# Two recurrent networks side by side: the first network's state update moved ahead of the second's gate sums on VectorE, and the second bf16 part of the state taken by GpSimd

## The chip, the cores and the metric

The kernel runs on one core of one Trainium2 chip. The metric is the device time of one execution in microseconds (us). A core has five engines that run their own programs and meet through semaphores: TensorE (PE in the rows; PEld is its weight load), VectorE (DVE), ScalarE (ACT), GpSimd (POOL) and SyncE (SP, which starts transfers here).

## The reference, cut to what matters

The whole program is a decoder of four layers, twelve stages. Only the first piece of the first stage is touched: two LSTM networks (one gives queries, one gives keys) that run over the same normalised input, 8 sequences of 112 positions with 256 features, with a state of 256.

```python
def _lstm(x, Wih, Whh, b):
    xW = jnp.einsum('bsd,gd->sbg', x, Wih) + b
    h0 = jnp.zeros((x.shape[0], Whh.shape[1]), x.dtype)
    def step(carry, xt):
        h, c = carry
        gates = xt + h @ Whh.T
        i, f, g, o = jnp.split(gates, 4, axis=-1)
        c = jax.nn.sigmoid(f) * c + jax.nn.sigmoid(i) * jnp.tanh(g)
        h = jax.nn.sigmoid(o) * jnp.tanh(c)
        return ((h, c), h)
    _, hs = jax.lax.scan(step, (h0, h0), xW)
```

Each of the 112 steps needs the state of the step before it, for each network. The two networks (l = 0 and l = 1 in the code) do not depend on each other.

## The kernel before, in words

`Recurrence` holds the stage. The input part `xW` of all gates is computed first (until about 70 us). Then 112 steps t follow, with both networks in each. The state is kept transposed: 128 partitions by 16 (two halves of 256 features, 8 sequences).

The product `h @ Whh.T` needs nearly fp32 accuracy and is made of bf16 matmuls. The state is split into three parts, each the upper 16 bits of an fp32 number: `h[:, 0]` is the state itself, `h[:, 1]` is what its upper half leaves out, and `h[:, 2]` what the upper half of `h[:, 1]` leaves out. `upper` is the bf16 view of the upper halves. The weights are split into three bf16 parts as well. For one network and one step TensorE runs three groups of 16 matmuls (L1323), named `part` 2, 1 and 0: part 2 reads only `h[:, 0]`, part 1 also `h[:, 1]`, part 0 also `h[:, 2]`. So the first group waits for the state (`h_hi`), the second for the middle part (`h_mid`), the third for the last (`h_parts`). TensorE's program is network 0's 48 matmuls, then network 1's 48, then the next step. The sixth gate block of the last group signals `gates_full`, the eighth signals it again.

VectorE sums the four slots of PSUM for the first six gate blocks and then for the last two (`dve_gates`, TENSOR_REDUCE at L1422, 48 and 16 outputs per partition). ScalarE takes tanh of both (L1352, L1355; the sigmoids are made from tanh) and writes the next step's input part to PSUM (L1366). VectorE makes the cell (`dve_cells`, L1428 and L1431), ScalarE its tanh (L1359), and VectorE the new state `h[:, 0]` (`dve_state`, L1440, signals `h_hi`). In the kernel before, VectorE then also makes `h[:, 1]` (`dve_middle`, L1446, signals `h_mid`), and GpSimd makes `h[:, 2]` (L1383, signals `h_parts`) and a halved copy of the state for later stages (L1385, signals `h_kept`, which the same network's next state waits for).

The order of each engine's program is written out by hand and is kept strictly: an instruction that waits holds back everything behind it on its engine. In VectorE's program of one step, network 1's first sum stands between network 0's cell and network 0's state.

Of the kernel before, what the change touches and what calls it, by code (L numbers as in the profile page):

```python
# [313 lines left out]
def norm_half_dve(k, half, src, xn, xT, before):  # L314

    norm_half_rows(k, half, src, xn, before)
    norm_half_turned(k, xT, before)
# [28 lines left out]
def norm_half_pool(k, before):  # L346
    s, G, st = k.s, k.nc.gpsimd, k.stats4
    G.wait_ge(*s.stat_ready(before + 1))
    G.tensor_tensor(st[:, :, 9], st[:, :, 8], k.minus_half[0:S, :].broadcast_to([S, HALF]),
                    ALU.pow).then_inc(*s.rstd_ready.up())  # L350
# [17 lines left out]
class Attention:  # L368
# [433 lines left out]
    def pool(self):  # L802
        k, s, G = self.k, self.s, self.nc.gpsimd
        self.pool_begin()
        norms = 0
        for step, b, i in self.order():
            u = self.bufs[b % 2]
            if step in ("stats", "ln", "stats3"):
                norms += 1
                G.wait_ge(*s.stat_ready(norms))  # L810
                G.tensor_tensor(k.stats[:, 9:10], k.stats[:, 8:9], k.minus_half[0:S, :],  # L811
                                ALU.pow).then_inc(*s.rstd_ready.up())
            elif step == "qm":
                G.wait_ge(*s.q_ready(b + 1))
                tiles, per = self.q.shape[1], self.qm.shape[1]
                for t in range(tiles):
                    ins = G.tensor_tensor(u["qm"][:, t * per:(t + 1) * per, :],
                                          self.q[:, t, :].unsqueeze(1).broadcast_to([P, per, S]),
                                          self.qm.unsqueeze(2).broadcast_to([P, per, S]), ALU.mult)
                ins.then_inc(*s.qm_ready.up())  # L820
            else:
                self.pool_more(step, b, i, u)
# [431 lines left out]
class Recurrence:  # L1254
# [113 lines left out]
    def pool(self):  # L1368
        k, s, G = self.k, self.s, self.nc.gpsimd
        for half in range(2):  # L1370
            norm_half_pool(k, half)
        G.wait_ge(*k.landed["l0a_whh"].now())
        for l in range(2):
            G.wait_ge(*s.whh_a(2 * l + 1))
            G.tensor_tensor(self.raw[:, l], self.raw[:, l], self.whh[:, 0, l], ALU.subtract).then_inc(*s.whh_g.up())
            G.wait_ge(*s.whh_a(2 * l + 2))
            G.wait_ge(*s.whh_g(2 * l + 1))
            G.tensor_tensor(self.whh[:, 2, l], self.raw[:, l], self.whh[:, 1, l], ALU.subtract).then_inc(*s.whh_g.up())
        for t in range(S):
            for l in range(2):  # L1380
                h, upper = self.h[:, l], self.upper[l]
                G.wait_ge(*s.h_mid(2 * t + l + 1))
                G.tensor_tensor(h[:, 2], h[:, 1], upper[:, 1], ALU.subtract).then_inc(*s.h_parts.up())  # L1383
                G.wait_ge(*s.h_hi(2 * t + l + 2))
                G.tensor_scalar(self.hs[:, l, :, :, t], self.h[:, l, 0].rearrange("p (k b) -> p k b", k=KD), 0.5, None,  # L1385
                                ALU.mult).then_inc(*s.h_kept.up())

    def dve(self):
        k, s, V, GT = self.k, self.s, self.nc.vector, self.GT
        for half in range(2):  # L1390
            norm_half_dve(k, half, k.x, self.xn, k.xnT[:, :, half * HALF:(half + 1) * HALF, :], half)
        V.wait_ge(*k.landed["l0a_bias"].now())
        for half in range(2):
            for n in range(2 * GT):
                l, g = divmod(n, GT)
                at = 2 * GT * half + n
                V.wait_ge(*s.up_full(at + 1))
                dst = self.xW[:, l].rearrange("p t (g b) -> p g b t", g=GT)[:, g, half * HALF:(half + 1) * HALF, :]
                V.tensor_scalar(dst, k.bank(at % 4, P, HT).rearrange("p (b t) -> p b t", b=HALF),  # L1399
                                self.bias["b_lstm"][:, n:n + 1], 1.0 if g in (4, 5) else 0.5, ALU.add,  # L1400
                                ALU.mult).then_inc(*s.gates_sum.up())
        V.memset(self.gates, 0.0)
        V.memset(self.h, 0.0).then_inc(*s.h_hi.up())
        V.wait_ge(*s.h_hi(1))
        for t in range(S):
            self.dve_gates(t, 0, 0, 6)
            self.dve_gates(t, 0, 6, 8)
            self.dve_cells(t, 0)
            self.dve_gates(t, 1, 0, 6)
            self.dve_state(t, 0)  # L1410
            self.dve_middle(t, 0)
            self.dve_gates(t, 1, 6, 8)
            self.dve_cells(t, 1)
            self.dve_state(t, 1)
            self.dve_middle(t, 1)

    def dve_gates(self, t, l, first, end):
        s, V = self.s, self.nc.vector
# [15 lines left out]
    def dve_state(self, t, l):  # L1434
# [3 lines left out]
        if t:  # L1438
            V.wait_ge(*s.h_kept(2 * t + l - 1))
        V.scalar_tensor_tensor(out=self.h[:, l, 0], in0=self.gates[:, l, 4], scalar=1.0, in1=self.tc[:, l], op0=ALU.add,  # L1440
                               op1=ALU.mult).then_inc(*s.h_hi.up())

    def dve_middle(self, t, l):
        s, V, h, upper = self.s, self.nc.vector, self.h[:, l], self.upper[l]
        V.wait_ge(*s.h_hi(2 * t + l + 2))
        V.tensor_tensor(h[:, 1], h[:, 0], upper[:, 0], ALU.subtract).then_inc(*s.h_mid.up())  # L1446


class Causal(Attention):
# [2189 lines left out]
```

## Time and profile before

| | |
|---|---|
| time, median of 3 runs | 2405.28 us (2404.35 to 2410.61) |
| time of the profiled execution | 2405.75 us |
| its span, first to last instruction | 2404.4 us |
| recurrence (112 steps), in that span | about 70 to 435 us |
| TensorE busy in the span | 2025.9 us (84%) |
| VectorE busy in the span | 1382.9 us (58%) |
| ScalarE busy | 896.4 us (37%) |
| GpSimd busy | 446.0 us (19%) |

Outside the span lie 1.35 us of the profiled execution. TensorE's busy time counts overlapped, modelled matmul durations, so it shows that matmuls are in flight and not that the array is at its peak.

### The profile page before, as it was taken

How to read it: one execution, taken by the hardware profiler on the slowest of the kernel's cores; microseconds unless marked ns; L12 is line 12 of the kernel's file. 1: busy time of each engine (PE TensorE's matmuls, PEld its weight loads, DVE VectorE, ACT ScalarE, POOL GpSimd, SP SyncE). 2: the span in 40 equal slices, each digit the busy share in tenths (PEclk: the TensorE clock that was granted, in tenths of full speed). 3: DMA queues.
4: the chain of work that ended last, by engine and by line, in shares of the span. 5: the costliest groups of instructions: out<-in, count | busy, mean ns of one | idle time of the engine just before them, and what ended most of it. 6: DMA issues, size and time to landing. Idle time of an engine off the chain costs nothing.

```text
span 2404.4 us, 57205 instructions
## 1 busy us (share of the span) xinstructions
PE 2025.9 (84%) x22720; PEld 1476.1 (61%) x22720; DVE 1382.9 (58%) x3825; ACT 896.4 (37%) x3421; POOL 446.0 (19%) x893
## 2 busy tenths in 40 slices
PE   7888888898987799898976887998999998789644
PEld 3788888786656566566865654665654545566422
DVE  5666666574435688544635624776261401678787
ACT  2444444353236466201324422655111111256411
POOL 3222222221101100101324512231000000400011
PEclk9655555799998899898998988999999998889856
DMA  3000000104000000300020000000030000000000
GB/s 131 4 4 4 4 4 5 74 2 169 7 1 2 14 11 5 132 1 22 1 94 33 1 1 10 8 11 1 1 146 1 0 0 1 8 11 11 1 0 16
DMA packets 7752, 57.19 MB, mean 24 GB/s; under 512 B 761, under 2 KB 5217, under 8 KB 5729
## 3 DMA queue, kind: packets, MB, share of 16 engines
q1 hardware_dynamic: 7488, 53.54, 5.8%
q8 instruction: 183, 3.00, 0.5%
q14 instruction: 81, 0.66, 0.1%
HBM read 52.62 MB, written 0.92 MB: 22 GB/s over the span
## 4 chain that ended last, share of the span: by engine, by line
PE 71%; DVE 11%; issue 9%; POOL 4%; ACT 2%; DMA 2%; POOLq 0%; DVEq 0%; ACTq 0%; SPq 0%
PE banks L259 41%; PE banks L1323 13%; PE banks L264 8%; PE banks L908 3%; PE banks L934 2%; DMA memory<-in_ctxT 1%; DVE memory L795 1%; PE banks L1480 1%; DVE memory L1218 1%; DVE memory L994 1%; DVE memory L1440 1%; ACT memory L956 1%; DVE memory L1002 1%; DVE memory L785 1%; PE banks L1631 1%
## 5 line engine op out<-in xcount | busy, mean ns | idle before, releaser
L259 PE MATMUL banks<-memory 128*112 128x256 f32 (+7 forms) x4192 | 1134.3, 427 | 69.8 <-POOL memory L2002 8.0
L259 PEld LDWEIGHTS banks<-memory 128*128 128x128 f32 (+3 forms) x4192 | 708.5, 196 | 399.8 <-issue 257.5
L264 PE MATMUL banks<-memory 112*125 112x112 f32 (+3 forms) x2000 | 309.5, 288 | 150.4 <-DVE memory L795 92.7
L264 PEld LDWEIGHTS banks<-memory 112*125 112x125 f32 (+3 forms) x2000 | 239.9, 173 | 268.7 <-issue 137.8
L1323 PE MATMUL banks<-memory 128*128 128x8 bf16 (+2 forms) x10752 | 307.0, 174 | 57.0 <-DVE memory L1440 55.4
L1323 PEld LDWEIGHTS banks<-memory 128*128 128x128 bf16 x10752 | 295.7, 104 | 69.0 <-DVE memory L1440 66.9
L956 ACT ACTIVATE memory<-banks,memory 112x375 f32<-112x375 f32 x384 | 215.4, 579 | 26.3 <-DVE memory L994 26.1
L994 DVE TENSOR_REDUCE memory<-banks 112x2 f32<-112x750 f32 x192 | 171.1, 934 | 47.5 <-PE banks L908 45.7
L1422 DVE TENSOR_REDUCE memory<-banks 128x48 f32<-128x192 f32 x448 | 119.5, 287 | 41.1 <-PE banks L1323 25.6
L1002 DVE COPY memory<-banks 125x448 f32<-125x448 f32 x192 | 116.6, 619 | 14.0 <-PE banks L264 9.9
L1352 ACT ACTIVATE memory<-memory 128x48 f32<-128x48 f32 x224 | 54.4, 243 | 136.7 <-DVE memory L1422 136.7
L1508 ACT ACTIVATE memory<-memory 112x112 f32<-112x112 f32 x192 | 71.7, 375 | 89.2 <-DVE memory L1529 89.2
L1383 POOL TENSOR_TENSOR memory<-memory 128x16 f32<-128x16 f32 x224 | 49.8, 222 | 279.2 <-DVE memory L1446 279.2
L978 ACT COPY memory<-banks 125x448 f32<-125x448 f32 x96 | 51.1, 533 | 129.7 <-PE banks L264 129.7
L908 PE MATMUL banks<-memory 32*112 32x375 f32 x768 | 88.4, 530 | 8.6 <-ACT memory L956 6.3
L811 POOL TENSOR_TENSOR memory<-memory 112x1 f32<-112x1 f32 x72 | 39.7, 551 | 298.9 <-DVE memory L790 297.5
L3114 DVE TENSOR_TENSOR memory<-banks,memory 112x256 f32<-112x256 f32 x8 | 3.4, 425 | 158.4 <-PE banks L259 158.4
L1201 ACT ACTIVATE memory<-banks,memory 112x112 f32<-112x112 f32 x256 | 86.4, 391 | 8.3 <-DVE memory L1218 6.9
L1366 ACT COPY banks<-memory 128x48 f32<-128x48 f32 x448 | 80.1, 179 | 23.6 <-DVE memory L1399 23.6
L3091 ACT ACTIVATE memory<-banks,memory 128x448 f32<-128x448 f32 x32 | 20.3, 635 | 173.5 <-PE banks L259 173.5
L956 ACT ACTIVATION_READ_ACCUMULATOR memory<-banks,memory 112x1 f32 x384 | 80.6, 210 | 0.0
L1034 POOL COPY memory<-memory 112x256 f32<-112x256 f32 (+1 forms) x40 | 19.6, 489 | 322.7 <-DVE memory L1007 311.0
(232 smaller groups left out, 2405.4 us busy)
## 6 DMA issues: line engine op xcount, KB each, us to landing
memory<-in_l2x SPq DMA_DIRECT2D x1, 7680.0 KB, 20.9
memory<-in_l2f SPq DMA_DIRECT2D x1, 7168.0 KB, 19.9
memory<-in_l1f SPq DMA_DIRECT2D x1, 4617.0 KB, 15.6
memory<-in_ctxT SPq DMA_DIRECT2D x24, 187.5 KB
memory<-in_l0a SPq DMA_DIRECT2D x1, 4224.0 KB, 15.9
memory<-in_l2f SPq DMA_DIRECT2D x1, 4096.0 KB, 12.8
memory<-in_l3f SPq DMA_DIRECT2D x1, 3073.0 KB, 22.7
memory<-in_l2a SPq DMA_DIRECT2D x1, 3072.0 KB, 19.9
```

The source lines that it names most:

```text
L259: ins = self.nc.tensor.matmul(out, weights[i], acts[i], start=i == 0, stop=i == n - 1)
L264: return self.nc.tensor.transpose(out, in_, self.ident[0:n, 0:n])
L908: ins = PE.matmul(k.bank(bank, S, CK), q, kT, start=True, stop=True)
L956: self.nc.scalar.activation(self.P_both[gi % 2][:, r, :], self.k.bank(r, S, CK), ACT.Exp, bias=u["nmax"][:, 4 * i + r:4 * i + r + 1], scal ...
L994: V.tensor_reduce(u["nmax"][:, 4 * i + 2 * h:4 * i + 2 * h + 2], k.banks[0:S, 2 * h:2 * h + 2, 0:CK], AX, ALU.max, negate=True).then_inc(* ...
L1002: V.tensor_copy(self.PT_both[gi % 2][0:CR, c, :], k.bank(k.at["turn", gi, c], CR, 4 * S)).then_inc(*s.pt_v.up())
L1201: A.activation(self.P_all[:, i, g, :], k.bank(i, S, 4 * S)[:, g * S:(g + 1) * S], ACT.Exp, bias=u["nmax"][:, 4 * i + g:4 * i + g + 1], sca ...
L1323: ins = self.nc.tensor.matmul(own[:, part:3, at:at + B], whh[:, part, l, j, g * P:(g + 1) * P], self.upper[l][:, 0:3 - part, j * B:(j + 1) ...
L1352: A.activation(self.gates[:, l, 1:4, :].rearrange("p g c -> p (g c)"), self.sums[:, l, 0:6 * B], ACT.Tanh).then_inc(*s.act_tanh.up())
L1366: self.nc.scalar.copy(self.slots[l][last][:, 3, :], src).then_inc(*self.s.xw_in.up())
L1422: V.tensor_reduce(self.sums[:, l, first * B:end * B], self.slots[l][last].rearrange("p s c -> p c s"), AX, ALU.add).then_inc(*s.gates_in.up())
L1508: A.activation(weights, weights, ACT.Exp, bias=self.nmax[n % 2][:, at:at + 1], scale=1.0, accum_out=self.total[n % 2][:, at:at + 1]).then_ ...
```

## The change

VectorE's program of a step is put in another order, and one of its instructions goes to GpSimd. `dve_state(t, 0)` now stands directly behind `dve_cells(t, 0)`, ahead of both gate sums of network 1. `dve_middle` is gone. GpSimd's part of a step and network is three instructions: the middle part (waits for `h_hi`), the last part (waits for GpSimd's own `h_mid`), and the kept copy. TensorE's and ScalarE's programs and all waits of TensorE are unchanged.

```diff
         for t in range(S):
             for l in range(2):
                 h, upper = self.h[:, l], self.upper[l]
+                G.wait_ge(*s.h_hi(2 * t + l + 2))
+                G.tensor_tensor(h[:, 1], h[:, 0], upper[:, 0], ALU.subtract).then_inc(*s.h_mid.up())
                 G.wait_ge(*s.h_mid(2 * t + l + 1))
                 G.tensor_tensor(h[:, 2], h[:, 1], upper[:, 1], ALU.subtract).then_inc(*s.h_parts.up())
-                G.wait_ge(*s.h_hi(2 * t + l + 2))
                 G.tensor_scalar(self.hs[:, l, :, :, t], self.h[:, l, 0].rearrange("p (k b) -> p k b", k=KD), 0.5, None,
                                 ALU.mult).then_inc(*s.h_kept.up())
...
             self.dve_gates(t, 0, 0, 6)
             self.dve_gates(t, 0, 6, 8)
             self.dve_cells(t, 0)
+            self.dve_state(t, 0)
             self.dve_gates(t, 1, 0, 6)
-            self.dve_state(t, 0)
-            self.dve_middle(t, 0)
             self.dve_gates(t, 1, 6, 8)
             self.dve_cells(t, 1)
             self.dve_state(t, 1)
-            self.dve_middle(t, 1)
...
-    def dve_middle(self, t, l):
-        s, V, h, upper = self.s, self.nc.vector, self.h[:, l], self.upper[l]
-        V.wait_ge(*s.h_hi(2 * t + l + 2))
-        V.tensor_tensor(h[:, 1], h[:, 0], upper[:, 0], ALU.subtract).then_inc(*s.h_mid.up())
```

On VectorE, one step's worth of the kernel before, from network 0's cell to network 1's middle part (banks are PSUM, memory is SBUF; the waits are the signals named above, `vstep` is VectorE's own):

```order
L1431 SCALAR_TENSOR_TENSOR memory<-memory 128x16 [waits vstep]
L1422 TENSOR_REDUCE memory<-banks 128x48 [waits gates_full,xw_in]
L1440 SCALAR_TENSOR_TENSOR memory<-memory 128x16 [waits h_kept,tc_ready,act_tanh]
L1446 TENSOR_TENSOR memory<-memory 128x16 [waits h_hi]
L1422 TENSOR_REDUCE memory<-banks 128x16 [waits gates_full,xw_in]
L1428 SCALAR_TENSOR_TENSOR memory<-memory 128x32 [waits act_tanh]
```

The same place of the changed kernel, where lines behind the edit carry a number lower by one:

```order
L1430 SCALAR_TENSOR_TENSOR memory<-memory 128x16 [waits vstep]
L1439 SCALAR_TENSOR_TENSOR memory<-memory 128x16 [waits h_kept,tc_ready,act_tanh]
L1421 TENSOR_REDUCE memory<-banks 128x48 [waits gates_full,xw_in]
L1421 TENSOR_REDUCE memory<-banks 128x16 [waits gates_full,xw_in]
L1427 SCALAR_TENSOR_TENSOR memory<-memory 128x32 [waits act_tanh]
```

The state (L1440, now L1439) went ahead of the sum of 48, and the two sums of network 1 now stand together with nothing between them.

On GpSimd, the first step of both networks before:

```order
L1383 TENSOR_TENSOR memory<-memory 128x16 [waits h_mid]
L1385 TENSOR_SCALAR memory<-memory 128x16 [waits h_hi]
L1383 TENSOR_TENSOR memory<-memory 128x16 [waits h_mid]
L1385 TENSOR_SCALAR memory<-memory 128x16 [waits h_hi]
```

and now:

```order
L1383 TENSOR_TENSOR memory<-memory 128x16 [waits h_hi]
L1385 TENSOR_TENSOR memory<-memory 128x16 [waits h_mid]
L1386 TENSOR_SCALAR memory<-memory 128x16
L1383 TENSOR_TENSOR memory<-memory 128x16 [waits h_hi]
L1385 TENSOR_TENSOR memory<-memory 128x16 [waits h_mid]
L1386 TENSOR_SCALAR memory<-memory 128x16
```

GpSimd has a third instruction per network and step, L1383 now makes the middle part, and L1385 the last part.

## Rows read from the trace of the kernel before

**Rows 1.** Busy time by stage: us, then each engine's busy us (instructions), clock, DMA.

```profile
70.00:435.00 365.00, 306.99 (x10752) 295.64 (x10752) 249.71 (x1344) 176.05 (x1118) 105.59 (x448) 0.50 0.02 4
```

**Rows 2.** The chain that ended last, one step: start us, us, what.

```profile
202.39 0.07 DVE memory L1422
202.46 0.19 issue
202.65 0.18 DVE memory L1440
202.82 0.04 issue
202.87 2.75 PE banks L1323 x96
```

**Rows 3.** Timeline of one step: start us, us, engine, line, what [idle before].

```profile
201.09 0.49 DVE L1422 TENSOR_REDUCE memory<-banks 128x48 f32<-128x192 f32 x2
...
202.19 0.21 ACT L1359 ACTIVATE memory<-memory 128x16 f32<-128x16 f32 x1 [0.26 <-DVE memory L1431]
...
202.37 0.36 DVE L1422 TENSOR_REDUCE memory<-banks 128x48 f32<-128x192 f32 x1 [0.21 <-PE banks L1323]
202.65 0.17 DVE L1440 SCALAR_TENSOR_TENSOR memory<-memory 128x16 f32<-128x16 f32 x1
...
202.85 0.17 DVE L1446 TENSOR_TENSOR memory<-memory 128x16 f32<-128x16 f32 x1
...
202.87 2.74 PE L1323 MATMUL banks<-memory 128*128 128x8 bf16 x96 [0.50 <-DVE memory L1440]
...
203.07 0.18 DVE L1428 SCALAR_TENSOR_TENSOR memory<-memory 128x32 f32<-128x32 f32 x1
203.10 0.23 POOL L1383 TENSOR_TENSOR memory<-memory 128x16 f32<-128x16 f32 x1 [1.61 <-DVE memory L1446]
...
203.29 0.17 DVE L1431 SCALAR_TENSOR_TENSOR memory<-memory 128x16 f32<-128x16 f32 x1
203.30 0.29 POOL L1385 TENSOR_SCALAR memory<-memory 128x16 f32<-128x16 f32 x1
...
203.50 0.22 ACT L1359 ACTIVATE memory<-memory 128x16 f32<-128x16 f32 x1
...
203.80 0.18 DVE L1440 SCALAR_TENSOR_TENSOR memory<-memory 128x16 f32<-128x16 f32 x1 [0.34 <-ACT memory L1359]
...
205.60 0.36 DVE L1422 TENSOR_REDUCE memory<-banks 128x48 f32<-128x192 f32 x1 [0.21 <-PE banks L1323]
...
206.10 2.06 PE L1323 MATMUL banks<-memory 128*128 128x8 bf16 x71 [0.50 <-DVE memory L1440]
...
207.56 0.49 DVE L1422 TENSOR_REDUCE memory<-banks 128x48 f32<-128x192 f32 x2
```

**Rows 4.** Costliest groups, TensorE's of the recurrence: busy, mean ns, idle before.

```profile
L1323 PE MATMUL banks<-memory 128*128 128x8 bf16 (+2 forms) x10752 | 307.0, 174 | 57.0 <-DVE memory L1440 55.4
```

**Rows 5.** One line's instructions: VectorE's states, min/median/max ns, first and last start.

```profile
L1440 DVE SCALAR_TENSOR_TENSOR memory<-memory x224: 165/174/176, 72.8 to 434.1; 128x16 f32<-128x16 f32 x112
```

**Rows 6.** Timeline around 94 us, VectorE behind an interrupted step.

```profile
93.96 0.17 DVE L1446 TENSOR_TENSOR memory<-memory 128x16 f32<-128x16 f32 x1
...
94.05 0.35 DVE L1422 TENSOR_REDUCE memory<-banks 128x48 f32<-128x192 f32 x1
```

**Rows 7.** Timeline of a later stage, GpSimd waiting for its own result.

```profile
1251.19 0.72 POOL L2244 TENSOR_TENSOR memory<-memory 112x256 f32<-112x256 f32 x1 [0.53 <-DVE memory L795]
1251.99 0.72 POOL L2246 TENSOR_TENSOR memory<-memory 112x256 f32<-112x256 f32 x1
```

**Rows 8.** Timeline of a later stage, TensorE released by GpSimd.

```profile
715.47 0.66 POOL L2002 TENSOR_TENSOR memory<-memory 128x224 f32<-128x224 f32 x1 [2.79 <-DVE memory L1236]
...
716.18 0.47 PE L259 MATMUL banks<-memory 128*112 128x256 f32 x1 [0.82 <-POOL memory L2002]
```

**Rows 9.** One line's instructions: VectorE's cells, min/median/max ns.

```profile
L1431 DVE SCALAR_TENSOR_TENSOR memory<-memory x224: 174/174/176, 72.3 to 433.5; 128x16 f32<-128x16 f32 x112
```

**Rows 10.** Timeline of the first step, still at the full TensorE clock.

```profile
70.00 2.55 PE L1323 MATMUL banks<-memory 128*128 128x8 bf16 x96 [1.41 <-DVE memory L1403]
...
71.39 0.49 DVE L1422 TENSOR_REDUCE memory<-banks 128x48 f32<-128x192 f32 x2 [1.53 <-PE banks L1323]
```

## The prediction, made before the changed kernel was run

> **What bounds the kernel now.** I read the busy times by stage first. The recurrence fills 365 us of the span; TensorE has matmuls in flight for 307 of them, VectorE works for 250, GpSimd for 106, and the granted clock is 0.50, which is the lower level, 1.2 GHz [rows 1]. No engine is full, so this stage is ruled by what waits for what. The change touches nothing outside it.
>
> The chain that ended last shows the pattern of one step [rows 2]: both networks' 96 matmuls (2.75 us), then VectorE's sum L1422, then the state L1440, then the matmuls again. The 0.19 us called "issue" is the sum's own run time. So the chain goes through the sum of network 1, although the next matmuls are network 0's and need only network 0's state. The timeline says why [rows 3]. Network 0's tanh of the cell starts at 202.19 and takes 0.21, so it ends at 202.40. Its state could follow, but VectorE has begun the sum of network 1 at 202.37, when TensorE finished network 1's sixth block, and reaches the state at 202.65. TensorE starts at 202.87, with 0.50 us idle before it. The next step repeats this 3.23 us later (206.10 less 202.87). Those 3.23 are a closed loop: TensorE to the sum of network 1 (205.60 less 202.87 = 2.73), sum to state (202.65 less 202.37 = 0.28), state to TensorE (0.22).
>
> **The state ahead of the sum.** This opens that loop. Three others remain, and the longest one gives the new step.
>
> Loop 1, one network alone. Sum to cell tanh is 202.19 less 201.09 = 1.10. Cell tanh to state, where nothing stands ahead of the state, is seen at network 1: 203.80 less 203.50 = 0.30. State to TensorE is 0.22, and 0.01 more because a state that starts on an idle VectorE takes 0.18 instead of 0.17. TensorE's start to the sum of 48 for the same network is 207.56 less 206.10 = 1.46 [rows 3]. Together 1.10 + 0.30 + 0.23 + 1.46 = 3.09. Network 1 has the same loop: its two sums now follow each other directly, as network 0's do.
>
> Loop 2, TensorE alone: 96 matmuls 0.027 apart (2.74 less one matmul's 0.17 of [rows 4], over 95) are 2.6 us. It no longer binds, and TensorE idles about 0.2 to 0.3 ahead of each network's block.
>
> Loop 3, VectorE's order. State 0, sum of network 1, its state, sum of network 0, state 0. Each state now holds back the other network's sum. A sum started 0.09 behind the 16-wide instruction ahead of it, when all that it waited for was there [rows 6]; I take 0.10 since a state follows a later release than that one. Then 2 × (0.10 + 1.40) = 3.00, just under loop 1.
>
> The new step is therefore 3.09, a gain of 0.14 on each of the 111 intervals between network 0's first and last state: 15.5 us. The count is from the 224 states, 72.8 to 434.1 us [rows 5].
>
> What is given back once, at the end: network 1's last state now comes 0.10 + 1.40 = 1.50 behind network 0's; before it was 203.80 less 202.65 = 1.15. That costs 0.35.
>
> **The middle part to GpSimd.** VectorE loses 224 instructions of 0.17. They cost it nothing now, except that network 1's second sum waited behind one; that is in loop 1 already. GpSimd gains 224 of about 0.22, by its own L1383, the same operation on the same shape [rows 3]. The time of arrival matters. GpSimd starts 0.08 after a VectorE instruction ends (202.85 + 0.17 to 203.10). So with the state's start as zero: middle part 0.26 to 0.48; then its own semaphore, 0.08 (1251.19 + 0.72 to 1251.99, [rows 7]); last part 0.56 to 0.78; kept copy 0.20 behind the last part's start, as now (203.30 less 203.10), and 0.29 long: 0.76 to 1.05. TensorE sees GpSimd's signal 0.05 after the end (715.47 + 0.66 to 716.18, [rows 8]): the middle part at 0.53, the last at 0.83. TensorE starts the network at 0.23, its second group 16 × 0.027 = 0.43 later at 0.66, its third at 1.09. Both arrive in time, by 0.13 and 0.26. Is 0.13 enough notice? Network 1's state in the kernel before ends at 203.98, is seen 0.05 later at 204.03, and its block begins 48 × 0.027 behind 202.87, at 204.17: 0.14 of notice, and the 96 matmuls run as one piece without a gap [rows 3]. So I cost this edit at nothing on the path. If the cover were gone, each 0.01 of lateness would add 0.01 to loop 1, 1.1 us in all. Queued behind GpSimd's new wait for `h_hi` are only the last part and the copy of the same network, and the other network's state comes 1.5 later, when GpSimd has long been idle. The copy's signal `h_kept` is wanted 3.09 after the state and comes at 1.05. At the stage's end the copy finishes 0.1 later than now.
>
> **The sum.** 15.5 − 0.35 − 0.1 = 15.1 us. The profiled execution took 2405.75, so 2390.7; the median shown is 0.47 lower, so 2390.2.
>
> On the clock: after some 365 us with matmuls in flight 84% of the time, the granted clock is still 0.50 [rows 1]. The Trainium skill (TensorE: Matmul & The Clock Gate, Part 1: The HAM clock gate) says that a busy TensorE is granted the full clock and an idle one half. By that rule a stage this busy would run at the higher level, and this trace disagrees. What the higher level would give is a rival below.
>
> **The rivals.**
> TensorE wants the middle part earlier than I think. In the kernel before, it was seen at 202.85 + 0.17 + 0.05 = 203.07 for a group at 203.30, 0.23 ahead. If that much were needed, loop 1 would be 0.10 longer: 3.19, a gain of 0.04 × 111 = 4.4 less 0.45, 2401.3. For it: no row shows a part 1 with less notice. Against it: the block of network 1 with 0.14.
>
> The state holds back the sum by more than 0.10. The other bound is the 0.20 from a state to the middle part, which waits for that state (202.65 to 202.85). Loop 3 would be 2 × 1.60 = 3.20, a gain of 0.03, 2402.4. Against it: the sum does not use the state. Loop 3 overtakes loop 1 at 0.145.
>
> GpSimd blocks VectorE, and the kernel gets slower. With three instructions per network, GpSimd's run from 0.26 to 1.05 behind a state. Network 1's product L1428 comes 0.70 behind its sum (203.07 less 202.37), so 0.80 behind state 0: inside the kept copy, with 0.25 of it still to run. If VectorE had to wait for that, loop 1 would be 3.09 + 0.25 = 3.34, a loss of 0.11 × 111 = 12.2 plus 0.45: 2418. It decides from 0.14 of blocking per step. Against it: in the kernel before the cell L1431 at 203.29 begins while GpSimd's L1383 runs (203.10 to 203.33), and still takes 0.17; all 224 cells take 174 to 176 ns, with or without GpSimd beside them [rows 9]. It is GpSimd that pays: its copy beside that cell takes 0.29 [rows 3]. The Trainium skill (SBUF — State Buffer, SBUF: two separate sides) states the rule in full: VectorE instructions with two SBUF inputs and GpSimd instructions exclude each other, and the later one blocks entirely. By the rule the cell would have ended late; the trace does not show that.
>
> The clock rises. TensorE will be busier per us, about 2.74 of 3.09. The first step shows the full clock: matmuls to the sum in 1.39 instead of 1.46 [rows 10]. Loop 1 would be 3.02, a gain of 0.21 × 111 = 23.3 less 0.45, 2382.9. Against it: 84% did not lift it, and 89% is not much more.
>
> **How the numbers follow.** My forecast 0.72, its own range 2386 to 2394 (0.02 either way for the rounding of four terms is 2 us, and later stages may shift by as much again). Middle part late 0.07; VectorE's order 0.05; GpSimd blocks 0.06; clock rises 0.04; something in the later stages that moves the total by more than its share 0.06, either way. What a measurement of this kernel can tell is about 0.3%, 7 us. Faster: 0.72 + 0.04 + 0.04 of the last = 0.80. No change: 0.07 + 0.05 + 0.01 = 0.13. Slower: 0.06 + 0.01 = 0.07. The range takes in the forecast's own and reaches up to the two cases of no gain: 2385 to 2401.
>
> **What would show it.** Right: network 0's states 3.08 to 3.10 apart; state 0.30 behind its cell tanh in both networks; the sum of network 1 directly behind state 0; TensorE idle ahead of network 1's block too; no gap within a block of 48. Wrong: a gap in TensorE in front of the 16-column matmuls that GpSimd's L1383 released (middle part late); cells or products over 0.2 us long, or starting late behind ScalarE's tanh (GpSimd blocks); the sum more than 0.14 behind the state; a granted clock of 1.00 inside the stage.

## The result, and the profile after

The changed kernel takes 2392.16 us (median of 6 runs, 2386.55 to 2395.0), against 2409.87 us for the kernel before in its 6 runs: a ratio of 0.9926, 95% interval 0.9909 to 0.9943. It is faster by 0.74%. The forecast was 2390.2 us, a ratio of 0.9937 to the median it started from. The profiled executions stand at 2405.75 and 2392.91 us, 12.8 us apart.

The medians are 17.7 us apart, about 5 more than the profiled executions. Which part of the program that comes from is not shown. The times of one kernel scatter by more than 5 us, and the shorter executions have the higher mean granted clock: of the changed kernel, 2386.55 us at 0.859 and 2395.0 us at 0.852.

Now the stage as a whole, the 112 steps of the kernel after, with the columns of [rows 1]:

```profile
71.40:424.30 352.90, 325.61 (x10752) 303.83 (x10752) 223.44 (x1120) 164.58 (x1118) 149.62 (x672) 0.51 0.02 5
```

From the view of single lines, the kernel after (answers to [rows 5]): VectorE's states, and the separate waits in its program, which DVEq, its sequencer, carries out.

```profile
L1439 DVE SCALAR_TENSOR_TENSOR memory<-memory x224: 174/174/177, 74.2 to 423.2; 128x16 f32<-128x16 f32 x112
...
L1438 DVEq EVENT_SEMAPHORE  x222: 452/454/457, 76.8 to 422.7; - x111
...
L1420 DVEq EVENT_SEMAPHORE  x448: 21/21/49, 72.7 to 421.8; - x150
```

From the first state to the last it is now 349.0 us; before it was 361.3 [rows 5]. So 12.3 of the 12.8 us come from this stage. TensorE's matmuls are in flight for 92% of it instead of 84% [rows 1], and the granted clock is 0.51, almost throughout the lower level, 1.2 GHz.

The chain that ended last, one step of one network (answers to [rows 2]):

```profile
202.21 0.23 ACT memory L1359
202.43 0.04 DVEq L1438
202.47 0.04 issue
202.51 0.18 DVE memory L1439
202.70 0.05 issue
202.75 1.47 PE banks L1323 x48
204.21 0.35 DVE memory L1421
204.57 0.02 issue
204.59 0.25 ACT memory L1352
```

The chain no longer runs through both blocks of TensorE and the other network's sum. It is one network alone: 48 matmuls, its sum, its tanh, and so on to its state. That is loop 1 of the prediction.

The timeline of one step of the kernel after (answers to [rows 3]; L1439 is the state, L1421 the sum, L1427 the product of the cell, L1383 the middle part, L1385 the last part, L1386 the kept copy):

```profile
202.21 0.22 ACT L1359 ACTIVATE memory<-memory 128x16 f32<-128x16 f32 x1 [0.27 <-DVE memory L1430]
...
202.51 0.17 DVE L1439 SCALAR_TENSOR_TENSOR memory<-memory 128x16 f32<-128x16 f32 x1 [0.34 <-ACT memory L1359]
202.67 0.49 DVE L1421 TENSOR_REDUCE memory<-banks 128x48 f32<-128x192 f32 x2
202.74 1.36 PEld L1323 LDWEIGHTS banks<-memory 128*128 128x128 bf16 x48 [0.17 <-DVE memory L1439]
202.77 0.22 POOL L1383 TENSOR_TENSOR memory<-memory 128x16 f32<-128x16 f32 x1 [0.78 <-DVE memory L1439]
...
203.07 0.22 POOL L1385 TENSOR_TENSOR memory<-memory 128x16 f32<-128x16 f32 x1
...
203.25 0.27 POOL L1386 TENSOR_SCALAR memory<-memory 128x16 f32<-128x16 f32 x1
...
203.34 0.19 DVE L1427 SCALAR_TENSOR_TENSOR memory<-memory 128x32 f32<-128x32 f32 x1 [0.18 <-ACT memory L1352]
...
204.08 0.17 DVE L1439 SCALAR_TENSOR_TENSOR memory<-memory 128x16 f32<-128x16 f32 x1 [0.34 <-ACT memory L1359]
204.20 0.49 DVE L1421 TENSOR_REDUCE memory<-banks 128x48 f32<-128x192 f32 x2
204.30 1.36 PEld L1323 LDWEIGHTS banks<-memory 128*128 128x128 bf16 x48 [0.21 <-DVE memory L1439]
...
205.60 0.17 DVE L1439 SCALAR_TENSOR_TENSOR memory<-memory 128x16 f32<-128x16 f32 x1 [0.34 <-ACT memory L1359]
```

Network 0's states are 3.09 apart (205.60 less 202.51), as forecast. The state starts 0.30 behind the start of its cell's tanh. The other network's sum follows a state by 0.16 or 0.12, more than the 0.10 that I had given it. It starts 1.46 behind the first weight load of its own network (204.20 less 202.74), which is the last term of loop 1: it waited for TensorE and not for the state, so it was loop 1 and not VectorE's order that ruled. The middle part is done 0.48 behind the state's start (202.77 + 0.22 less 202.51), and each block of 48 weight loads is one piece of 1.36, with 0.17 or 0.21 idle ahead of it in both networks (forecast 0.2 to 0.3).

What the prediction did not have is this, on VectorE, in the same trace some six us earlier:

```profile
196.03 0.17 DVE L1439 SCALAR_TENSOR_TENSOR memory<-memory 128x16 f32<-128x16 f32 x1 [0.34 <-ACT memory L1359]
196.49 0.49 DVE L1421 TENSOR_REDUCE memory<-banks 128x48 f32<-128x192 f32 x2 [0.28 <-PE banks L1323]
...
197.89 0.17 DVE L1439 SCALAR_TENSOR_TENSOR memory<-memory 128x16 f32<-128x16 f32 x1 [0.34 <-ACT memory L1359]
198.00 0.36 DVE L1421 TENSOR_REDUCE memory<-banks 128x48 f32<-128x192 f32 x1
```

The sum comes 0.46 behind network 0's state instead of 0.16. The profile names TensorE, which had long been done. This happens behind network 0's state in every eighth step, 14 times, and makes that step 3.39 instead of 3.09. In the kernel before there are five such steps, 0.21 to 0.25 longer than 3.23; [rows 6] stand behind one of them.

The account of the stage: predicted 111 × 0.14 = 15.5 less 0.35 for the last state. The interruptions took 14 × 0.30 = 4.2 instead of 5 × 0.24 = 1.2, which is 3.0 more. 15.5 − 0.35 − 3.0 = 12.1, measured 12.3.

### The profile page after: what moved, and what is told of

The parts are those of the page before. It is cut to its first block, busy times and chain, and to the rows that moved or that the text cites. A ratio compares the mean times of both kernels' runs of the same rounds, so it can differ in the third digit from the quotient of the medians.

```text
span 2391.6 us, 57205 instructions
## 1 busy us (share of the span) xinstructions
PE 2042.9 (85%) x22720; PEld 1481.5 (62%) x22720; DVE 1357.0 (57%) x3601; ACT 884.7 (37%) x3421; POOL 489.8 (20%) x1117
## 4 chain that ended last, share of the span: by engine, by line
PE 65%; DVE 16%; issue 10%; ACT 5%; POOL 4%; DMA 1%; DVEq 0%; POOLq 0%; ACTq 0%; SPq 0%
PE banks L259 42%; PE banks L264 8%; PE banks L1323 6%; PE banks L908 3%; PE banks L934 2%; DVE memory L1421 2%; ACT memory L1352 1%; ACT memory L1359 1%; DVE memory L795 1%; PE banks L1474 1%; DVE memory L1218 1%; DVE memory L1427 1%; DVE memory L1430 1%; DVE memory L1439 1%; ACT memory L956 1%
## 5 line engine op out<-in xcount | busy, mean ns | idle before, releaser
L1323 PE MATMUL banks<-memory 128*128 128x8 bf16 (+2 forms) x10752 | 325.6, 175 | 25.9 <-DVE memory L1439 5.8
L1323 PEld LDWEIGHTS banks<-memory 128*128 128x128 bf16 x10752 | 303.8, 104 | 48.3 <-DVE memory L1439 46.2
L1421 DVE TENSOR_REDUCE memory<-banks 128x48 f32<-128x192 f32 x448 | 109.4, 285 | 5.5 <-PE banks L1323 5.5
L1383 POOL TENSOR_TENSOR memory<-memory 128x16 f32<-128x16 f32 x224 | 48.5, 217 | 206.7 <-DVE memory L1439 206.7
L1034 POOL COPY memory<-memory 112x256 f32<-112x256 f32 (+1 forms) x40 | 19.6, 490 | 320.8 <-DVE memory L1007 309.1
L1439 DVE SCALAR_TENSOR_TENSOR memory<-memory 128x16 f32<-128x16 f32 x224 | 39.1, 175 | 75.8 <-ACT memory L1359 75.8
```

The lines of the kernel that those rows point to most:

```text
L1323: ins = self.nc.tensor.matmul(own[:, part:3, at:at + B], whh[:, part, l, j, g * P:(g + 1) * P], self.upper[l][:, 0:3 - part, j * B:(j + 1) ...
L1421: V.tensor_reduce(self.sums[:, l, first * B:end * B], self.slots[l][last].rearrange("p s c -> p c s"), AX, ALU.add).then_inc(*s.gates_in.up())
```

## The experiments

Nine runs were made, in three groups; the runs of a group were on the same chip, and each ratio is to the kernel before in the same group. Where a stage is told, it is from the first to the last state of VectorE in the profile: 361.3 us before, 349.0 after.

**The changed kernel again.**

> The changed kernel itself, timed beside the three below. Expected: 17 us (0.7%) under the kernel before, and in the profile again 3.09 us from one state of network 0 to the next, with an interruption of 0.30 us every 8 steps, 14 in all, behind network 0's state. Theory P (VectorE's own program): each interruption stands at a fixed place in VectorE's instruction stream, every 128 instructions, and a step of the changed kernel is 16 VectorE instructions with its separate waits, so the place is the same in every eighth step. Theory T (time): something that comes every 25 us whatever the program is.

Ratio 0.9932 (0.9911 to 0.9954), 2387.65 us against 2405.82. Its states run from 73.7 to 422.9, 349.2 us, with the same 14 interruptions. The medians are 18.2 us apart, again more than the stage gives.

**Two more instructions ahead of the loop.** A step is 10 VectorE instructions and 6 separate waits: 448 of L1420 and 222 of L1438 above, for 112 steps. That is 16, and 8 steps are 128. The kernel before has 18 in a step.

```diff
+        V.memset(self.tc, 0.0)
+        V.memset(self.prod, 0.0)
         V.memset(self.gates, 0.0)
         V.memset(self.h, 0.0).then_inc(*s.h_hi.up())
```

> The changed kernel with two more small memsets on VectorE ahead of the step loop (of buffers that are written before they are read). Theory P: the place of the interruption moves by two instructions, to behind network 0's cell and ahead of the wait for the cell's tanh, where VectorE waits 0.45 us anyway; the interruptions vanish from the pace: all steps 3.09, the recurrence 14 x 0.30 = 4.2 us shorter than in the changed kernel, less 0.3 for the memsets: profile near 2389. Theory T: 14 interruptions of 0.30 as before, 2393.

Theory P holds. The line of VectorE's states in this kernel:

```profile
L1441 DVE SCALAR_TENSOR_TENSOR memory<-memory x224: 174/175/176, 73.6 to 418.5; 128x16 f32<-128x16 f32 x112
```

344.9 us, 4.1 less than 349.0, and 344.9 less the 1.5 between the networks, over 111, is 3.09 with nothing left over for interruptions. Ratio to the kernel before 0.9917 (0.9899 to 0.9934), 2386.04 us. Theory T, 14 interruptions of 0.30 as before, falls.

**One more instruction instead of two** (the same edit with the memset of `tc` alone).

> The changed kernel with one more small memset on VectorE ahead of the step loop. Theory P: the interruption now stands between the separate wait for the cell's tanh and network 0's state itself. If it begins only when VectorE's program gets there it is fully on the path, 0.30 every 8 steps as in the changed kernel, with the state over 0.30 + 0.30 behind the cell's tanh in those steps. If fetching runs on during the wait, it is hidden as with two memsets and the recurrence is 4 us shorter. Theory T: 0.30 behind the state every 25 us, as in the changed kernel.

The interruption moved by one instruction, and it is on the path: network 0's state, in a disturbed step, comes 0.87 behind its cell (L1432) instead of 0.51, after 0.69 idle instead of 0.34.

```profile
170.88 0.17 DVE L1432 SCALAR_TENSOR_TENSOR memory<-memory 128x16 f32<-128x16 f32 x1
171.75 0.17 DVE L1441 SCALAR_TENSOR_TENSOR memory<-memory 128x16 f32<-128x16 f32 x1 [0.69 <-ACT memory L1359]
```

The line of its states:

```profile
L1441 DVE SCALAR_TENSOR_TENSOR memory<-memory x224: 174/174/176, 74.4 to 424.3; 128x16 f32<-128x16 f32 x112
```

The stage is 349.9 us, 14 interruptions of 0.35. So it is the place in VectorE's stream that counts. Here it stands behind the separate wait for the cell's tanh, and that wait did not hide it. There is one execution of this kernel, 2390.67 us; the reading rests on its trace.

**GpSimd's part alone.** VectorE's order as before:

```diff
             self.dve_cells(t, 0)
-            self.dve_state(t, 0)
             self.dve_gates(t, 1, 0, 6)
+            self.dve_state(t, 0)
             self.dve_gates(t, 1, 6, 8)
```

> One part of the change alone: the middle part by GpSimd, VectorE's order as before (network 1's sum ahead of network 0's state). My theory: the loop over both blocks of TensorE, network 1's sum and network 0's state is as it was, 3.23 us a step; the only gain or loss is in interruptions, 5 of 0.23 before, now 14 of up to 0.16: within 2 us of the kernel before, no measurable change. Rival (what helped is a VectorE with 224 instructions less): a good part of the 15 us appears here, steps near 3.1.

Ratio 0.9999 (0.9985 to 1.0013): nothing. The timeline of this kernel:

```profile
203.74 0.36 DVE L1421 TENSOR_REDUCE memory<-banks 128x48 f32<-128x192 f32 x1 [0.21 <-PE banks L1323]
204.01 0.17 DVE L1439 SCALAR_TENSOR_TENSOR memory<-memory 128x16 f32<-128x16 f32 x1
204.09 0.22 DVE L1421 TENSOR_REDUCE memory<-banks 128x16 f32<-128x64 f32 x1
...
204.23 1.93 PE L1323 MATMUL banks<-memory 128*128 128x8 bf16 x66 [0.49 <-DVE memory L1439]
```

The state is still behind the sum, TensorE still idles 0.49, and the step is 3.23. VectorE's 224 instructions less bought nothing. Of its interruptions I expected up to 0.16 each; they are 0.22, 14 times, and the stage is 1.6 us longer than before (73.6 to 436.5), which the timed runs do not tell from zero.

**The order alone.** The middle part stays on VectorE, behind its state, and both go ahead of the sum:

```diff
             self.dve_cells(t, 0)
+            self.dve_state(t, 0)
+            self.dve_middle(t, 0)
             self.dve_gates(t, 1, 0, 6)
-            self.dve_state(t, 0)
-            self.dve_middle(t, 0)
             self.dve_gates(t, 1, 6, 8)
```

> The other part alone: network 0's state and then its middle part ahead of network 1's sums, all on VectorE. My theory (loop 3): the middle part waits for the state it follows (0.20 from start to start), then the sum starts 0.09 behind it, so each network's sum comes 0.29 behind the other's state instead of 0.10. 2 x (0.29 + 1.40) = 3.38 us a step, 0.15 more than before: 111 x 0.15 = 17 us slower than the kernel before, plus 0.5 at the end, about 2423. Rival (the order alone carries the gain): steps near 3.09, 2391.

Ratio 1.0085 (1.0069 to 1.0102), 2429.21 us against 2407.71: slower by 0.85%. The timeline of this kernel:

```profile
201.42 0.18 DVE L1440 SCALAR_TENSOR_TENSOR memory<-memory 128x16 f32<-128x16 f32 x1 [0.34 <-ACT memory L1359]
201.63 0.18 DVE L1446 TENSOR_TENSOR memory<-memory 128x16 f32<-128x16 f32 x1
201.65 1.36 PEld L1323 LDWEIGHTS banks<-memory 128*128 128x128 bf16 x48 [0.34 <-DVE memory L1440]
...
201.72 0.48 DVE L1422 TENSOR_REDUCE memory<-banks 128x48 f32<-128x192 f32 x2
...
203.12 0.17 DVE L1440 SCALAR_TENSOR_TENSOR memory<-memory 128x16 f32<-128x16 f32 x1 [0.34 <-ACT memory L1359]
203.33 0.18 DVE L1446 TENSOR_TENSOR memory<-memory 128x16 f32<-128x16 f32 x1
```

State to middle part 0.21, middle part to sum 0.09, sum to the other network's state 1.40. The half step is 1.70, the step 3.40 (forecast 3.38). The states run from 73.3 to 454.2, a stage of 380.9 us, 19.6 longer than before where 17.5 were expected: 111 steps that are 0.02 longer than forecast make 2.2 of it. Loop 3 is real, and the change needs both of its parts: without GpSimd the new order loses 21 us, and without the order GpSimd gains none.

**The middle part later.** On GpSimd the kept copy goes ahead of the middle part:

```diff
                 G.wait_ge(*s.h_hi(2 * t + l + 2))
+                G.tensor_scalar(self.hs[:, l, :, :, t], self.h[:, l, 0].rearrange("p (k b) -> p k b", k=KD), 0.5, None,
+                                ALU.mult).then_inc(*s.h_kept.up())
                 G.tensor_tensor(h[:, 1], h[:, 0], upper[:, 0], ALU.subtract).then_inc(*s.h_mid.up())
                 G.wait_ge(*s.h_mid(2 * t + l + 1))
                 G.tensor_tensor(h[:, 2], h[:, 1], upper[:, 1], ALU.subtract).then_inc(*s.h_parts.up())
-                G.tensor_scalar(self.hs[:, l, :, :, t], self.h[:, l, 0].rearrange("p (k b) -> p k b", k=KD), 0.5, None,
-                                ALU.mult).then_inc(*s.h_kept.up())
```

> The changed kernel with GpSimd's kept copy ahead of the middle part instead of behind the last part, so that the middle part comes 0.20 us later (start to start of two GpSimd instructions). My theory: it had 0.13 us of notice at TensorE's second group, so it is 0.07 late; loop 1 is 3.16 a step, 111 x 0.07 = 8 us slower than the changed kernel (about 2400), and a gap of 0.07 opens in TensorE between the first and second group of 16 matmuls. Rival A (TensorE needs more notice than it shows): the loss is nearer 0.20 a step, 22 us. Rival B (the middle part never matters because loop 3 or something else rules): no loss.

Ratio 0.9978 (0.9966 to 0.999), 2404.08 us. The stage is 358.7 us (74.2 to 432.9), 9.7 longer than after, where 8 were expected. Half a step of this kernel:

```profile
201.55 1.81 PE L1323 MATMUL banks<-memory 128*128 128x8 bf16 x53 [0.34 <-DVE memory L1439]
201.59 0.27 POOL L1383 TENSOR_SCALAR memory<-memory 128x16 f32<-128x16 f32 x1 [1.16 <-DVE memory L1439]
201.80 0.21 POOL L1385 TENSOR_TENSOR memory<-memory 128x16 f32<-128x16 f32 x1
...
203.10 0.36 DVE L1421 TENSOR_REDUCE memory<-banks 128x48 f32<-128x192 f32 x1
```

The sum now comes 1.55 behind TensorE's start instead of 1.46, so the block is 0.09 longer. The middle part is ready for TensorE at 201.80 + 0.21 + 0.05 = 202.06 and was wanted at 201.55 + 0.43 = 201.98: 0.08 late. So TensorE needs no more notice than the arrival itself: rival A (0.20 a step) and rival B (nothing) both fall, and the 0.13 of slack in the prediction was real.

**A better version.** The chain after shows 0.04 of "DVEq L1438" and 0.04 of "issue" between the cell's tanh and the state. VectorE's state waits for two semaphores in the first step and for three later. The first one written rides on the instruction, and the others make a separate wait ahead of it. In the code the first is one that has long been met. In this version the late one is written first:

```diff
     def dve_gates(self, t, l, first, end):
...
-        V.wait_ge(*s.xw_in(2 * (2 * t + l) + 1 + last if t else 2 * l + 1 + last))
         V.wait_ge(*s.gates_full(2 * (2 * t + l) + 1 + last))
+        V.wait_ge(*s.xw_in(2 * (2 * t + l) + 1 + last if t else 2 * l + 1 + last))
...
     def dve_state(self, t, l):
         s, V = self.s, self.nc.vector
-        V.wait_ge(*s.act_tanh(2 * (2 * t + l) + 2))
         V.wait_ge(*s.tc_ready(2 * t + l + 1))
+        V.wait_ge(*s.act_tanh(2 * (2 * t + l) + 2))
```

The first of the two kernels has only the second piece. Both also have the two memsets.

> The kernel with two more memsets, and in the state update the two waits for ScalarE written in the other order: the wait for the cell's tanh first, then the one for the gates' tanh and the kept copy. The profiles show that the first wait written rides on the instruction and the others go into a separate one ahead of it; the state starts 0.30 us behind the start of the cell's tanh, of which 0.215 is the tanh, while instructions with one wait start 0.03 behind their releaser's end. My theory: loop 1 rules, so the state 0.06 earlier makes a step 3.03 instead of 3.09: 111 x 0.06 = 6.7 us less than with the memsets alone. Rival (loop 3 or TensorE's order is already just as long, or the separate wait costs nothing): steps stay within 0.01 of 3.09.

The stage is 338.7 us (73.6 to 412.3), 6.2 less than with the memsets alone (6.7 expected); 3.04 a step. There is one execution of it, 2385.02 us, so the reading rests on its trace.

> As the run before, and in the gate sums too the wait for TensorE is written first, so that it rides on the sum. A sum now starts 0.11 us behind the end of the sixth block's last matmul; with a wait that rides on it I expect about 0.05. My theory: loop 1 becomes 2.98 a step, 111 x 0.11 = 12 us less than with the memsets alone, near 2374 to 2377, and a measurable 1.2% to 1.3% under the kernel before. If only the state's wait counted, 3.03 and 2379 to 2382.

2377.2 us (4 runs) against 2406.9, ratio 0.9877 (0.986 to 0.9894). The lines of its states and of their separate wait, and then a state in its timeline:

```profile
L1441 DVE SCALAR_TENSOR_TENSOR memory<-memory x224: 174/176/177, 74.1 to 404.9; 128x16 f32<-128x16 f32 x112
...
L1440 DVEq EVENT_SEMAPHORE  x222: 50/50/50, 76.6 to 404.4; - x111
```

```profile
201.40 0.21 ACT L1359 ACTIVATE memory<-memory 128x16 f32<-128x16 f32 x1 [0.27 <-DVE memory L1432]
...
201.65 0.18 DVE L1441 SCALAR_TENSOR_TENSOR memory<-memory 128x16 f32<-128x16 f32 x1 [0.28 <-ACT memory L1359]
```

The stage is 330.8 us, 2.97 a step (forecast 2.98). The separate wait takes 0.05 and no longer 0.45, and the state comes 0.25 behind the tanh's start instead of 0.30. This version is 1.2% under the kernel before. It beats the changed kernel, and also the changed kernel with the memsets, timed beside it in the next run: the interval 0.986 to 0.9894 meets neither 0.9909 to 0.9943 nor 0.9908 to 0.994.

> The changed kernel with the two memsets once more, beside the two kernels above on one chip: 0.8% under the kernel before, steps 3.09 without an interruption.

Ratio 0.9924 (0.9908 to 0.994), where its first run had 0.9917. Its stage is as in that run (74.0 to 419.2, 345.2 us), yet its profiled execution is 2398.33 us against 2385.92 of the same kernel in the second experiment. The stretches from the end of the recurrence on, of the one and the other:

```profile
419.60:2384.60 1965.00, 1665.85 (x11824) 1153.33 (x11824) 1092.27 (x2415) 706.18 (x2290) 321.12 (x434) 0.91 0.06 24
...
420.30:2397.00 1976.70, 1672.10 (x11824) 1156.02 (x11824) 1091.94 (x2415) 706.06 (x2290) 321.34 (x434) 0.91 0.06 24
```

The same instructions take 11.7 us more, and TensorE's busy time 6 us more. The mean granted clock of the whole execution was 0.853 here and 0.855 there. The later stages scatter by that much from run to run. A few us of a change in the recurrence are therefore read from the stage in the profile, and not from the total; whether the two memsets are worth their 4 us in the total these timings do not settle.

## Why the prediction was right, point by point

- **What bounded the kernel** was right: loop over both blocks, the other network's sum and the state. Shown by GpSimd's part alone: with the old order the step stayed at 3.23.
- **Loop 1, 3.09** was right, and is the chain after. That it rules was shown twice: making it longer by 0.09 (sixth experiment) and shorter by 0.06 and 0.07 (the two kernels with the waits rewritten) moved the step by just that.
- **Loop 3, 3.00** was right in kind, and did not rule. Where a sum was late already, behind an interruption, it followed the state by 0.11 (197.89 to 198.00), which makes the loop 3.02. So the rival "the state holds back the sum", which needed more than 0.145, did not come true. With the middle part between state and sum the loop ruled at 3.40, and that would have made the change a loss if GpSimd had not taken the middle part. I had costed VectorE's relief as nearly nothing. By itself it is; together with the new order it is worth the difference between 3.40 and 3.09, and the prediction did not say that.
- **The middle part at nothing, 0.13 of slack** was right (sixth experiment).
- **0.35 given back at the end**: the last two states were 1.15 apart before; now they are 1.86 (421.35 and 423.21 in the trace after), of which 0.30 is the last interruption. The other 1.56 makes it 0.41 given back.
- **The term that was missing** is the interruptions, 3.0 us. The prediction saw one of them in the trace of before, took a price from the rows behind it, and did not ask what it was or how often it would come with another number of instructions in a step. It is why the stage gave 12.3 us and not 15. That the total still came close to the forecast is in part luck: the stage fell 3 us short, and the medians are 5 us further apart than the profiled executions.
- **GpSimd blocks VectorE** was wrong as a rival of 0.25. The prediction argued it away with cells, and the cell that it named shared only 0.04 with GpSimd's instruction (203.29 to 203.33 in [rows 3]), which says little. The product that the rival was about is the test. It did start inside the kept copy, at 203.34 with the copy running from 203.25 to 203.52, and took 0.19; the 224 products take 191 to 212 ns, the longest where they started 0.03 behind the copy. In the sixth experiment products (L1427) that started 0.01 behind a GpSimd subtraction took up to 0.25 instead of 0.19 (205.28 behind 205.27, for one), so there is some blocking, of 0.06, far under the 0.22 that the subtraction ran. The Trainium skill (SBUF — State Buffer, SBUF: two separate sides) has the later instruction blocked entirely; the trace shows a part.
- **The clock rises** did not happen. In the kernel after, the granted clock is 1.00 from 60.00 to 71.40, 0.71 on average from 71.40 to 80.00, where TensorE's matmuls are in flight for 7.77 of the 8.60 us, and 0.50 from 80.00 on; it stayed there with matmuls in flight 92% of the time. The Trainium skill (TensorE: Matmul & The Clock Gate, Part 1: The HAM clock gate) would have a busy TensorE at full clock; in no run here did the level rise again among these narrow matmuls.
- **A slip in a rival's price**: the time under "the clock rises" starts from the profiled 2405.75 and not, as the others do, from the median. From 2405.28 it is 2382.4 and not 2382.9; nothing hangs on it.

## What to carry to other kernels

With two independent chains on in-order engines, list the closed loops (each chain alone, each engine's order) and compute each one's period; moving an instruction ahead opens one loop and may close a longer one, so look at what follows the moved instruction and waits for it. Where an instruction waits for several semaphores, write the one that comes last first, and look in the trace whether a separate wait stands ahead of it. Count an engine's instructions per turn of a short loop: a pause at a fixed place in its stream can fall on the path at every eighth turn, or nowhere.

## What the runs showed of the hardware that I had not expected

VectorE's stream is interrupted by 0.3 to 0.35 us at a fixed place every 128 instructions, separate waits counted. In the kernel after, with 16 to a step, that is the same place in every eighth step; one memset more ahead of the loop moved it by one instruction, and two hid it. In the kernel before, with 18 to a step, it wanders and shows 5 times, by 0.21 to 0.25. The profile has an instruction queue with 81 packets and 0.66 MB, 8.1 KB each, and the Trainium skill (Perfetto Trace Analysis, The 4-stage abstract model) gives an instruction 64 bytes, so 128 of them are 8 KB. The start times of the packets go with VectorE's stream. In the trace after, one of 8192 bytes starts in each of the 14 interrupted steps, 1.06 to 1.35 us behind network 0's state, beside others of the queue that keep no such place. With the two memsets there is still one every eight steps, though no pause shows on the path, and in the kernel before there is one every seven or eight steps, as 128 over 18 would have it. Yet the packet starts only behind the pause (at 197.10, where the delayed sum began at 196.49), so the pause is not the time of that transfer. That it comes from passing from one such block to the next is argued from this, and not shown.

The wait that rides on an instruction and the wait that is issued separately differ by 0.05 to 0.07 us here, if it is the late one: the two places together were worth 0.12 of a 3.09 us step.
